# Gate, output projection, last norm, switch and feed-forward as one program by token blocks

## The reference, cut to what matters

```python
o = rwkv7_op(r, w, k2, v, -kk, kk * a)                       # the recurrence
o = (o.reshape(Bq, Tq, H, N) * gn_scale + gn_offset).reshape(Bq, Tq, Cq)
o = o + rwkv.reshape(Bq, Tq, Cq)
x = x + o * g @ W_o                                          # gate, output projection
y = layernorm(x)                                             # last norm
top_expert = argmax(softmax(y @ Wg.T))                       # switch, 2 experts
out0 = gelu(y @ W0a.T + b0a) @ W0b.T + b0b                   # feed-forward 0
out1 = relu(y @ W1a.T + b1a) @ W1b.T + b1b                   # feed-forward 1
x = x + out0 * mask0 + out1 * (1.0 - mask0)
```

## Time and profile before

| | us |
|---|---|
| median of 3 runs | 1370.47 (1370.43 to 1371.58) |
| the profiled execution | 1369.02 |
| its span, first to last instruction | 1367.2 |
| recurrence ends, first gate instruction | 1198.43 |
| first output projection on TensorE | 1201.22 |
| last norm's small instructions | 1227.99 |
| first transpose | 1231.45 |
| first switch product | 1238.72 |
| first feed-forward product | 1250.01 |
| last addition to `x` | 1362.18 |

### The profile page before, as it was taken

How to read it: one execution, slowest core, us unless ns; L and a number is a source line. 1 busy time by engine, 2 the same in 40 slices (tenths; PEclk the granted TensorE clock), 3 DMA queues, 4 the chain that set the end, 5 groups by cost and what they waited for, 6 DMA issues and landing times. The chain is left out here.

```text
span 1367.2 us, 32613 instructions
## 1 busy us (share of the span) xinstructions
PE 1235.5 (90%) x13048; PEld 707.2 (52%) x13048; DVE 857.5 (63%) x1709; ACT 564.3 (41%) x846; POOL 248.1 (18%) x444
## 2 busy tenths in 40 slices
PE   5879999999999999878999968995999999958998
PEld 2523333333333333264677643443888888844665
DVE  6377788888888888156333375896666666672212
ACT  2315777777777777732133224542111111103221
POOL 4220100100100010040377300334211111000000
PEclk9967999999999999999999979997999999978999
DMA  4310122111112210060153400002000000000000
GB/s 126 55 22 3 28 38 44 27 27 28 27 32 40 35 28 4 2 220 1 46 166 104 143 31 0 0 0 77 5 4 4 3 4 4 4 1 1 16 16 31
DMA packets 33838, 49.49 MB, mean 36 GB/s; under 512 B 11995, under 2 KB 22331, under 8 KB 32955
## 3 DMA queue, kind: packets, MB, share of 16 engines
q1 hardware_dynamic: 29211, 36.55, 11.8%
q0 software_dynamic: 3744, 10.23, 2.4%
q10 hardware_dynamic: 768, 1.05, 0.2%
HBM read 23.63 MB, written 9.31 MB: 24 GB/s over the span
## 5 line engine op out<-in xcount | busy, mean ns | idle before, releaser
L664 DVE TENSOR_REDUCE at_block_max<-at_p_ring 128x4 f32<-128x512 f32 x576 | 367.6, 685 | 76.1 <-PE at_p_ring L570 41.9
L641 ACT ACTIVATE at_probs<-at_p_score,abias 128x1024 f32<-128x1024 f32 (+2 forms) x320 | 318.8, 1029 | 122.8 <-PE at_p_score L600 68.6
L570 PE MATMUL at_p_ring<-kt,qt 64*128 64x128 bf16 (+3 forms) x1152 | 186.9, 284 | 10.0 <-PEq L727 7.3
L615 PE MATMUL at_p_out<-at_probs,at_vs 128*32 128x512 f32 (+3 forms) x1536 | 164.5, 500 | 0.4 <-ACT at_probs L641 0.4
L594 PE MATMUL at_p_score<-qt,kt 64*128 64x512 bf16 (+3 forms) x768 | 145.9, 331 | 5.7 <-ACT at_probs L641 4.8
L570 PEld LDWEIGHTS at_p_ring<-kt,qt 64*128 64x128 bf16 x1152 | 69.9, 95 | 130.5 <-DVE at_block_max L664 86.6
L707 POOL TENSOR_TENSOR at_shift<-shift,at_row_max 128x16 f32<-128x16 f32 x32 | 7.1, 220 | 422.9 <-DVE at_row_max L670 422.9
L594 PEld LDWEIGHTS at_p_score<-qt,kt 64*128 64x128 bf16 x768 | 38.3, 94 | 85.6 <-ACT at_probs L641 55.2
L2055 ACT COPY rc_ta<-rc_bank 128x256 f32<-128x256 f32 x32 | 10.3, 375 | 148.9 <-PE rc_bank L1826 148.9
L2295 DVE SCALAR_TENSOR_TENSOR x<-ff_p_out,branch,x 128x256 f32<-128x256 f32 x32 | 13.3, 476 | 87.2 <-PE ff_p_out L2251 87.2
L2260 PE MATMUL ff_p_in<-xt_ffn,w_in 128*128 128x512 f32 x128 | 61.3, 607 | 1.2 <-PEq L2185 1.2
(11 more groups left out here) (325 smaller groups left out, 2160.9 us busy)
## 6 DMA issues: line engine op xcount, KB each, us to landing
qt<-qparts SPq DMA_DIRECT2D x96, 64.0 KB, 2.4
kt<-kparts SPq DMA_DIRECT2D x96, 64.0 KB, 2.5
rows<-moe_chosen SPq DMA_DIRECT2D x4, 1024.0 KB, 4.8
w_routed<-in_w_routed_dram SPq DMA_DIRECT2D x1, 2816.0 KB
x<-in_x_dram SPq DMA_DIRECT2D x4, 512.0 KB, 8.3
moe_table<-rows SPq DMA_DIRECT2D x4, 512.0 KB, 2.7
out_dram<-x SPq DMA_DIRECT2D x4, 512.0 KB, 2.9
w_down<-in_w_down_dram SPq DMA_DIRECT2D x1, 1408.0 KB
```

What stands on the lines that cost most here:

```text
L570: mm = pe.matmul(bank[:, col:col + nb * P], qt[nxt][h * ROWS:(h + 1) * ROWS, pair, t * P:(t + 1) * P], kt[nxt][h * ROWS:(h + 1) * ROWS, pa ...
L615: mm = pe.matmul(p_out[32 * h:32 * h + 32, left(k):QC], vs[(now - e[2]) % BUFS][:, key, h, :], probs[g % PROBS][:, h % 2, at:at + w], star ...
L641: act.activation(probs[g % PROBS][:, :, 0:len(pairs) * w], p_score[g % 2][:, :, 0:len(pairs) * w], ACT.Exp, bias=abias[:, c * TPB + key:c ...
L664: dve.tensor_reduce(dst, src, AX.X, ALU.max).then_inc(s["fill_used"], 1)
```

## The change

The five programs become one, `finish_phase`. It goes by token blocks. The front part of a block is: gate, projection, sum with statistics, norm, transposes. The front parts of block 0 stand ahead of everything; the projection of block n+1 stands in block n's feed-forward behind its first narrow product, and its transposes stand behind the narrow product of m = 5. The norm's small instructions work on four tiles instead of 16, and three of their six waits are gone. The switch is computed with the turned tokens as weights and `w_switch` as the moving matrix of two columns: eight products a block instead of two of 512 columns, and the logits come out by token, so that the copy and the transposes back fall away. One pair of PSUM banks, `p_work`, holds projection, turned tiles and logits of a block in turn. ScalarE computes one square root per block (`root`), between the Gelu and the Relu tiles of the block before.

```diff
-        branch, xt = sb("branch", [P, TILES, 2]), sb("xt_ffn", [P, EH, NB, TB + 1])
-        gate_and_project(nc, data, vec, w_out, x, stats)
-        layernorm_stats(nc, "ln4_", x, stats, mean, rstd, eps)
-        normalise_and_turn(nc, "nt4_", x, mean, rstd, ident, xt)
-        switch_phase(nc, xt, w_switch, ident, branch)
-        switched_ffn_phase(nc, x, xt, branch, w_in, b_in, w_back, b_back, out)
+        finish_phase(nc, data, vec, w_out, x, stats, eps, ident, w_switch, w_in, b_in, w_back, b_back, out)
...
+            @block.tensor
+            def _(pe):
+                def project(n):
+                    pe.wait_ge(gated_ready, (n + 1) * EH)
+                    if n:
+                        pe.wait_ge(tok_read, n)
...
+                def turn(n):
+                    for j in range(2):
+                        pe.wait_ge(xn_ready, n * TPN + 2 * j + 2)
...
+                def switch(n):
+                    for t in range(TPN):
+                        for h in range(EH):
+                            mm = pe.matmul(p_work[:, 0, 2 * t:2 * t + 2], xt[n % 2][:, h, t * P:(t + 1) * P], w_switch[:, h, :],
+                                           start=h == 0 and t == 0, stop=h == EH - 1, skip_group_check=True)
+                    mm.then_inc(tok_ready, 1)
...
+                project(0)
+                turn(0)
                 for n in range(NB):
...
+                        widen(n, m)
+                        if m == 0:
+                            switch(n)
                         if m >= 1:
+                            narrow(n, m - 1)
+                        if m == 1 and n + 1 < NB:
+                            project(n + 1)
+                        if m == 6 and n + 1 < NB:
+                            turn(n + 1)
+                    narrow(n, HT - 1)
...
             @block.scalar
             def _(act):
+                def root(n):
+                    act.wait_ge(handed, 2 * n + 1)
+                    act.activation(std[:, :], var[:, :], ACT.Sqrt, bias=eps[:, 0:1]).then_inc(handed, 1)
...
+                root(0)
+                take(0)
                 for n in range(NB):
                     for m in range(HT):
...
                         act.activation(hidden[m % 2][:, :], p_in[m % 2][:, :], ACT.Gelu if m < FT else ACT.Relu,
                                        bias=b_in[:, m:m + 1]).then_inc(hidden_ready, 1)
+                        if m == FT and n + 1 < NB:
+                            root(n + 1)
+                        if m == 6 and n + 1 < NB:
+                            take(n + 1)
...
+                    c.mark(dve.tensor_tensor(half[:, :], some[:, :, 1], some[:, :, 4], ALU.add))
+                    c.mark(dve.tensor_tensor(diff[:, :], some[:, :, 1], some[:, :, 4], ALU.subtract))
+                    c.link(dve.tensor_tensor(var[:, :], some[:, :, 2], some[:, :, 5], ALU.add))
+                    c.mark(dve.tensor_scalar(mean[:, :], half[:, :], 0.5, None, ALU.mult))
+                    c.link(dve.scalar_tensor_tensor(diff[:, :], diff[:, :], 0.25, diff[:, :], ALU.mult, ALU.mult))
+                    dve.scalar_tensor_tensor(var[:, :], var[:, :], 1.0 / E, diff[:, :], ALU.mult, ALU.add).then_inc(handed, 1)
...
+                gate(0)
+                gate(1)
+                add_projection(0)
+                normalise(0)
+                for n in range(NB):
+                    choose(n)
+                    add_bias(n)
+                    if n + 1 < NB:
+                        add_projection(n + 1)
+                        normalise(n + 1)
+                    add_branch(n, 0)
+                    if n + 2 < NB:
+                        gate(n + 2)
+                    add_branch(n, 1)
```

More of the change, by code:

```diff
@@ L2107, in _ @@
                         y1(t + 1, b)
[L2110 to L2164, removed]
@@ L2170, with finish_phase @@
 TIE = 2.0 ** -25
-def switch_phase(nc, xt, w_switch, ident, masks):
+def finish_phase(nc, data, vec, w, x, stats, eps, ident, w_switch, w_in, b_in, w_back, b_back, out):
     with ExitStack() as ctx:
[L2176 to L2211, removed]
@@ L2214, in switched_ffn_phase @@
[L2214 to L2221, removed]
+        sb = lambda n, s, d=F32: ctx.enter_context(nc.sbuf_tensor("fi_" + n, s, d))
+        ps = lambda n, s, d=F32: ctx.enter_context(nc.psum_tensor("fi_" + n, s, d))
@@ new lines, in widen, with narrow @@
+                def widen(n, m):
+                    if m == 0:
+                        pe.wait_ge(taken, 2 * n + 2)
+                    if m >= 2:
+                        pe.wait_ge(hidden_ready, n * HT + m - 1)
+                    for h in range(EH):
+                        mm = pe.matmul(p_in[m % 2][:, :], w_in[:, h, m * P:(m + 1) * P], xt[n % 2][:, h, :], start=h == 0, stop=h == EH - 1)
+                    mm.then_inc(in_ready, 1)
+                def narrow(n, m):
+                    e = m // FT
+                    pe.wait_ge(hidden_ready, n * HT + m + 1)
+                    if m % FT == 0 and n:
+                        pe.wait_ge(out_used, (n - 1) * 2 + e + 1)
+                    for t in range(TPN):
+                        mm = pe.matmul(p_out[e][:, t, :], hidden[m % 2][:, t * P:(t + 1) * P], w_back[:, m, :],
+                                       start=m % FT == 0 and t % 2 == 0, stop=m % FT == FT - 1, skip_group_check=True)
+                    mm.then_inc(out_ready, 1)
@@ L2280, in _, with gate @@
                 c = Chain(dve, chain_s)
[L2281 to L2284 removed]
+                at = lambda n, t: x[:, n * TPN + t, :]
+                def gate(n):
+                    for h in range(EH):
+                        c.mark(dve.scalar_tensor_tensor(gated[n % 2][:, h, :], rows("yt", h, n), v_("gn_scale", h), rows("bonus", h, n),
+                                                        ALU.mult, ALU.add))
+                    c.wait()
+                    for h in range(EH):
+                        dve.scalar_tensor_tensor(gated[n % 2][:, h, :], gated[n % 2][:, h, :], v_("gn_offset", h), rows("gt", h, n),
+                                                 ALU.add, ALU.mult).then_inc(gated_ready, 1)
@@ new lines, in add_branch @@
+                def add_branch(n, e):
+                    dve.wait_ge(out_ready, n * HT + (e + 1) * FT)
+                    for t in range(TPN):
+                        c.mark(dve.scalar_tensor_tensor(at(n, t), p_out[e][:, t, :], branch[n % 2][:, t, e:e + 1], at(n, t), ALU.mult, ALU.add))
+                    c.wait()
+                    dve.sem_inc(out_used, 1)
+                gate(0)
[12 more added lines that the diff above has]
+                    add_branch(n, 1)
```

107 lines of the change are left out of this document (63 added, 44 removed).

## The result

The changed kernel takes 1361.57 us (median of four runs, 1360.91 to 1361.94) against 1370.45 for the kernel before on the same chip: a ratio of 0.9929 (the two medians alone give 0.9935), 95% interval 0.9917 to 0.9941. It is faster by about 9 us, more than the 0.2% that can be told from no change, and 6.1 us slower than the 1355.5 that was forecast, though within the range.

The account below looks back on a forecast made before the run. Bound by the chain across engines up to 1250.01 us, then TensorE alone. 35.06 - 10.4 - 2.6 - 7.1 = 15.0 us off 1369.02 gives 1354.0; with 1.45 for the median, 1355.5; range 1350 to 1362, about 0.85.

Parts of the forecast that it names:

- the forecast's own case: Whole kernel: the measured time lies within 3 us of the forecast sum, 1355.5 us; chance 0.70.
- Part 1: Block 0's front, ahead of the feed-forward: the first feed-forward product starts at 1214.95 instead of 1250.01, 35.06 us earlier.
- Part 2: Work added to TensorE's feed-forward stretch: three projections 10.4 us, transposes 2.6, four switches 7.1 (bounds 4.0 and 14.2).
- Part 3: Later blocks' fronts, hidden under the feed-forward on other engines: cost nothing, with 4.6 us of slack at the transposes.
- the feed-forward's cold start: Half clock at the start of block 0's feed-forward: costs 1.9 us as before; earlier transposes might save 0 to 2.6.
- the falling clock: Rival: the switch lowers TensorE's clock once in every block, 1361 to 1368 us, taken as 1362; chance 0.08.
- The uncovered front: Rival: TensorE waits at three blocks' transposes; fully exposed 28 us, 1384; chance 0.03 under 9.6 us late, 0.03 later.
- the cheap switch: Rival: switch loads take 62 ns, saving 3.1 us, and the clock is up early, saving 1.9: 1350.5 us; chance 0.11.
- the switch that costs twice: Rival: the switch's loads and products don't overlap, 7.1 us more, 1362.6 us; chance 0.05.

Follow-up runs that it names:

- e5: Changed kernel with the next block's projection, transposes, root and copies placed behind the whole feed-forward: 1391.63 us, ratio 1.014.
- e4: Changed kernel with unread products in both front waits and block 0's switch moved behind the first narrow product: 1354.98 us, ratio 0.9880.
- e9: The same kernel as e4, profiled once more: 1361.72 us in one execution.
- e2: Changed kernel with five unread products between block 0's first projection and its first transposes: 1354.51 us, ratio 0.9878.
- e1: Changed kernel with only block 0's switch moved behind the first narrow product: 1358.76 us, ratio 0.9907.
- e6: Changed kernel with ScalarE's root of the next block behind the Relu of m = 6 instead of m = 4: 1367.68 us, ratio 0.9962.

## Why the prediction was right, and where it was off

The time lies in the range, but only 0.4 us inside its upper edge, and the forecast's own case, the sum within 3 us, did not come true. Which way the time goes, what bounds it and all terms but one were right; the clock was not.

**What bounds the kernel** was read rightly: a chain across engines up to 1250, TensorE alone behind it.

**Part 1** forecast 16.5 us from the first gate to the first feed-forward product; it is 16.7. The six small instructions take 0.82 us from 1213.36 to the root at 1214.18, where 0.9 was worked out.

**Part 2** is right to 0.3 us: the kernel whose clock never falls takes 130.6 us for the stretch, the sum without cold start says 130.3. The switch at 111 ns a record, priced from L1059 and not from the 62 ns of L2195, costs 1.78 us, so of the two bounds the row of the same weight form was the right one. By an estimate from what the Trainium skill ("TensorE: Matmul & The Clock Gate", section "LDWEIGHTS (loading the stationary operand)") gives for 128 columns, 16 loads take 1.7 us. The trace agrees: the 16 records take 1.68 us.

**Part 3** is right: no wait of TensorE in the stream. The table loads of block 0 lie at 1243.98 and 1256.25, both under TensorE's work; the timeline of the kernel after at the first:

```profile
1243.98 1.28 ACT L2216 ACT_TABLE_LOAD   x1
...
1245.27 0.30 ACT L2216 ACTIVATE fi_std<-fi_var,eps 128x4 f32<-128x4 f32 x1
...
1251.68 1.04 PE L2167 MATMUL fi_p_work<-ident,fi_xn 128*128 128x128 f32 x8
```

From the root's start to the transposes it is 6.4 us here, of which VectorE needs 1.9: 4.5 us of slack, where 4.6 was worked out.

**The step that failed** is the one line of the sum that says "the feed-forward's cold start (1.9 us) is kept", with bounds of 0 and 2.6 us. It cost 5.9 (half of 11.85). I had carried it over from a place in which only wide products followed. In the changed kernel the second thing that TensorE does is the switch, and I had seen that it "lets the array do nearly nothing", but used it only for a rival in which a full clock falls, not for the term that it stretches. The row that I held against that rival, L1059, streams 80 columns a load; the switch streams two. With 5.9 instead of 1.9 the sum gives 11.0 us. The 1.9 was not impossible: in the kernel with the front behind the feed-forward (e5) two of four cold starts cost about that, because the clock rose just ahead of the switch. But nothing in the forecast priced the case in which it doesn't.

The rest, 3.0 us in that one execution, lies ahead of all that was changed. In the profiles of the ten experiments and the two of the comparison the first gate instruction starts anywhere between 1198.06 and 1208.40 us, though what runs before is the same. Two profiles of one kernel (e4 and e9, waits filled and switch moved) lie 8.0 us apart, and the earliest of all, 1198.06, is a kernel with the change in it (e2, one wait filled). In the kernel after, the attention's first score products start at 82.1 us instead of 79.2. The profile of before was an early one, second of the twelve, and its time lies 1.45 us below its median, which the forecast added; that may be the same scatter. So scatter covers the 3.0 us; a small cost of the change in that part is not excluded, since before has one profile only.

Of the rivals, the falling clock named the two columns of the switch but put the loss in another place, a full clock that falls in every block. Its 1362 us lie next to the 1361.57 measured, and that is luck: once up, the clock never fell. The uncovered front, tried by placing it behind the feed-forward, came out slower, +30 us against the 28 worked out for it, and that nearness is luck too: the 28 were waiting alone, and measured were 20.2 us of waiting and 9.6 of cold starts; the cheap switch and the switch that costs twice were both refuted by 1.78 us.

## What to carry to other kernels

Where a chain across engines stands ahead of a stage bound by TensorE, splitting by token blocks and running a block's chain inside its neighbour's products turns all but the first chain into cover: here it was worth 30 us against the same program without overlap. A cold start is not a constant: look at which products stand in it. Here 16 records of two moving columns in it made it 11.9 us long, and moving them behind it made it 4.3. Or fill the waits ahead of it with wide products that nobody reads (here 9 us for eight products). In working out such a sum, give the clock a term of its own, half of the time that TensorE works at half clock, and bounds for a rise that comes ahead of the odd products and for one that comes behind them: here 1.8 and 5.9 us.

## What the runs showed of the hardware that I had not expected

- The share of time that the profile calls busy did not tell where TensorE's clock would stand. With 16 records of two moving columns among wide products it stayed at 1.2 GHz for 11.85 us of 100% busy, with 48 of them for 18.4 us of the stream, until 1237; 48 in a row at full clock brought it down 2.6 us behind their start.
- In one program the clock rose 3.0 us behind the first wide product at two starts, just ahead of the 16 short records, and 11.9 and 12.1 us behind it at the two where the short records came first.
- A single switch of 1.7 us was followed by a fall of a full clock, 3.4 us long, in block 0 when it stood behind the first narrow product and the front's waits were filled (three profiles of three), but not in the same place without the filling (e1, one profile), never in blocks 1 to 3, and not in any block when it stood behind the first `p_in` (two profiles with a full clock, seven more with the clock full from block 1 on). Why was not settled.
- A table load of 1.28 us is followed by its activation within 0.02 us, between a Relu and a square root (loads at 1243.98 in the changed kernel and 1251.98 in e6).
- The part of the program ahead of the change varied by up to 10 us between profiled executions of kernels that are the same up to there (1198.06 to 1208.40), and by 8 us between two of one kernel.
